# Two states per GpSimd product, channel-major tiles from the convolution, dt products in two row groups, and the skip term in two halves

## What is computed

```python
xz = x @ w_in.T
xi, z = jnp.split(xz, 2, axis=-1)                 # 256 channels each
xc = silu(depthwise_conv3x3(xi) + conv_b)
# four directions: by rows, by columns, and both of them backwards
x_dbl = jnp.einsum('bkdl,kcd->bkcl', xs, x_proj_w)        # 8 + 16 + 16 rows
dts, Bs, Cs = jnp.split(x_dbl, [8, 24], axis=2)
dts = jnp.einsum('bkrl,kdr->bkdl', dts, dt_w)
delta = softplus(dts + dt_b)
# along the 65536 tokens of a direction, for each of 16 states n:
h = exp(delta * A[n]) * h + delta * x * B[n]
y = sum_n(h * C[n]) + Ds * x
# the four y are added in the order of the picture, normed, gated by silu(z)
out = x + (layernorm(y) * silu(z)) @ w_out.T
```

## Time and profile before

| | |
|---|---|
| median of 3 runs | 27252.67 us (27248.71 to 27273.89) |
| profiled execution, span | 27255.4 us |
| VectorE (DVE) busy | 25541.9 us, 94% |
| TensorE (PE) busy | 24154.8 us, 89% |
| ScalarE (ACT) busy | 23950.4 us, 88% |
| GpSimd (POOL) busy | 22732.5 us, 83% |

### The profile page before, as it was taken

How to read it: one execution, slowest core, us unless ns; L and a number is a source line. 1 busy time by engine, 2 the same in 40 slices (tenths; PEclk the granted TensorE clock), 3 DMA queues, 4 the chain that set the end, 5 groups by cost and what they waited for, 6 DMA issues and landing times. The chain is left out here.

```text
span 27255.4 us, 517756 instructions
## 1 busy us (share of the span) xinstructions
PE 24154.8 (89%) x189836; PEld 20228.8 (74%) x189836; DVE 25541.9 (94%) x25237; ACT 23950.4 (88%) x47871; POOL 22732.5 (83%) x17291
## 2 busy tenths in 40 slices
PE   3998789999999989999999888888888888888889
PEld 1776457777777777777777777777777777777777
DVE  7999999999999999999999999999999999999996
ACT  2777459999999999999999999999999999999996
POOL 0000029999999999999999999999999999999996
PEclk7999899999999999999999999999999999999999
DMA  4112333333333344444444434344444444444435
GB/s 162 51 52 75 94 102 134 134 133 135 133 134 132 134 143 148 144 147 144 147 145 146 141 140 142 141 141 142 142 141 140 145 148 144 148 146 145 148 136 199
DMA packets 1529381, 3677.49 MB, mean 135 GB/s; under 512 B 105908, under 2 KB 1156952, under 8 KB 1247192
## 3 DMA queue, kind: packets, MB, share of 16 engines
q1 hardware_dynamic: 1526872, 3644.42, 38.3%
HBM read 3055.75 MB, written 588.25 MB: 134 GB/s over the span
## 5 line engine op out<-in xcount | busy, mean ns | idle before, releaser
L1198 POOL TENSOR_TENSOR s_prod<-s_h,s_cb 128x1024 f32<-128x1024 f32 x8192 | 19555.5, 2387 | 537.3 <-DVE s_h L1166 384.6
L1166 DVE TENSOR_TENSOR_SCAN s_h<-s_da,s_h,s_db 128x512 f32<-128x512 f32 x16256 | 19365.7, 1259 | 534.5 <-PE s_db L1070 497.4
L1127 ACT ACTIVATE s_da<-s_delta,a_neg 128x512 f32<-128x512 f32 x16384 | 10856.6, 712 | 1100.6 <-DVE s_h L1166 1100.4
L1116 ACT ACTIVATE s_dxb<-s_dx,s_btok 128x256 f32<-128x256 f32 x24576 | 10621.5, 498 | 53.1 <-PEq L57 53.1
L1067 PE MATMUL s_db<-eye,s_dxb 128*128 128x128 f32 x49152 | 8273.2, 277 | 2195.0 <-issue 1419.1
L1067 PEld LDWEIGHTS s_db<-eye,s_dxb 128*128 128x128 f32 x49152 | 5605.3, 142 | 4356.4 <-issue 3152.6
L1083 PE MATMUL s_py<-eye,s_prod 128*128 128x128 f32 x65536 | 8494.6, 273 | 10.2 <-POOL s_prod L1198 9.7
L1083 PEld LDWEIGHTS s_py<-eye,s_prod 128*128 128x128 f32 x65536 | 7432.8, 142 | 13.0 <-POOL s_prod L1198 13.0
L1070 PE MATMUL s_db<-s_bdiag,s_dx 128*128 128x128 f32 x32768 | 6338.9, 275 | 0.0
L1070 PEld LDWEIGHTS s_db<-s_bdiag,s_dx 128*128 128x128 f32 x32768 | 4951.9, 191 | 0.0
L1183 POOL TENSOR_SCALAR s_bdiag<-eye,s_btok 128x128 f32<-128x128 f32 x8192 | 3172.1, 387 | 226.9 <-POOLq L57 226.9
(11 more groups left out here) (132 smaller groups left out, 16852.9 us busy)
## 6 DMA issues: line engine op xcount, KB each, us to landing
s_cb<-c_rows SPq DMA_DIRECT2D x2048, 1024.0 KB, 4.7
s_xt<-xc_tok SPq DMA_DIRECT2D x1024, 256.0 KB, 5.3
y<-s_yt SPq DMA_DIRECT2D x1024, 256.0 KB
s_yb<-y SPq DMA_DIRECT2D x768, 256.0 KB, 4.5
xc_own<-s_xc SPq DMA_DIRECT2D x256, 512.0 KB, 3.4
s_xc<-xc_own SPq DMA_DIRECT2D x256, 512.0 KB, 5.6
xc_tok<-c_ot SPq DMA_DIRECT2D x32, 2048.0 KB, 8.5
o_y<-y SPq DMA_DIRECT2D x64, 1024.0 KB, 6.2
```

What stands on the lines that cost most here:

```text
L1116: last = e.activation(dxb[:, i % NDXB, j, :], dx[:, g % 2, j, :], ACT.Copy, scale=btok[:, g % 2, j, n:n + 1])
L1127: last = e.activation(da[:, i % NDA, half, :], delta[:, g % 2, half, :], ACT.Exp, scale=wts[k]["a_neg"][:, half, n:n + 1])
L1166: last = e.tensor_tensor_scan(h[:, n, half, flow], da[:, i % NDA, half, flow], db[:, i % NDB, half, flow], first, ALU.mult, ALU.add)
L1198: e.tensor_tensor(prod[:, i % NP_], h[:, n], cb[:, n, :].unsqueeze(1).to_broadcast([P, HALVES, T]), ALU.mult).then_inc(S["prod"], 1)
```

## The change

In `scans_phase`:

- GpSimd multiplies the two states of a pair (TOGETHER = 2) in one instruction of 2048 elements a partition; prod has three buffers of two states. Its scalings stay single and are issued up to two pairs ahead. A product waits for both scans. LAG goes from 2 to 4, so totals and y come two steps later; AHEAD stays 2.
- Only direction 1 (`turned_in`) transposes its tiles and stores them. Direction 0 reads channel-major tiles from xc_own[0], as the backward directions do.
- The projection has 73 output rows: the 9 rows of dt once more from row 64 on. Both halves of dt are formed in stage 6, the first from rows 0 to 8, the second from rows 64 to 72 of low and of dt_w, each into its own bank.
- The skip term's two halves of the channels are divided: half 0 in direction 2, half 1 in direction 3.
- Stage 11 waits for the token-major tile itself, since stage 0 is no longer there to do it.

In `conv_phase`, SP stores eight finished rows of xc to xc_own[0] in two DMAs (one a half) ahead of the store of xc_tok, and ScalarE waits for these stores before it writes the ring again.

```diff
+DT_AGAIN = ROWS_LOW
+ROWS_ALL = DT_AGAIN + DT_RANK + 1
...
+        def kept_again(e, r):
+
+            if r >= RING:
+                e.wait_ge(S[f"own{r // 8 % 2}"], HALVES * DMA * (r // RING))
...
+                        finished(e, r)
+                        tiles = slice((r - 7) * SIDE // BANK, (r + 1) * SIDE // BANK)
+                        for half in range(HALVES):
+                            e.dma_start(xc_own[0, tiles, :, half, :].rearrange("t p f -> p t f"),
+                                        xc[:, half, here:here + 8, :].rearrange("p (t r) w -> p t (r w)", r=BANK // SIDE)
+                                        ).then_inc(S[f"own{r // 8 % 2}"], DMA)
...
+                        kept_again(e, PAIR * q)
...
+                            kept_again(e, STRIP * c)
...
-    NDA, NDXB, NDB, NP_ = 3, 3, 2, 3
-    AHEAD, LAG = 2, 2
+    NDA, NDXB, NDB = 3, 3, 2
+    TOGETHER, GROUPS_KEPT = 2, 3
+    AHEAD, LAG = 2, 4
     SUBS_ACT = 3
     STEPS = TILES * D_STATE
-    SKIP = 2
+    SKIP = {2: 0, 3: 1}
     backwards = lambda k: k >= 2
     by_column = lambda k: k % 2 == 1
+    turned_in = lambda k: k == 1
...
-        prod = m.sb("s_prod", [P, NP_, HALVES, T])
+        prod = m.sb("s_prod", [P, GROUPS_KEPT, TOGETHER, HALVES, T])
...
-                    last = e.matmul(pr[0:ROWS_LOW, 0, :], w["proj"][:, half, :], xc[:, s, half, :],
+                    last = e.matmul(pr[0:ROWS_ALL, 0, :], w["proj"][:, half, :], xc[:, s, half, :],
...
-                e.matmul(pr[:, 0, :], w["dt_w"][:, 0:P], low[0:DT_RANK + 1, :], start=True, stop=True).then_inc(S["dts"], 1)
             elif stage == 6:
                 e.wait_ge(S["btok"], n)
-                e.matmul(pr[:, 1, :], w["dt_w"][:, P:2 * P], low[0:DT_RANK + 1, :], start=True, stop=True).then_inc(S["dts"], 1)
+                for half, at in enumerate((0, DT_AGAIN)):
+                    rows = slice(at, at + DT_RANK + 1)
+                    e.matmul(pr[:, half, :], w["dt_w"][rows, half * P:(half + 1) * P], low[rows, :],
+                             start=True, stop=True).then_inc(S["dts"], 1)
...
                 e.wait_ge(S["delta"], n)
+                e.wait_ge(S[f"load{s}"], LINES * DMA * ((n + 1) // 2))
...
+                e.dma_start(xc[:, 0], own(0, 0)).then_inc(S["xld0"], DMA)
                 load(e, 0, 0)
-                e.wait_ge(S["xc"], 1)
-                e.dma_start(own(0, 0), xc[:, 0]).then_inc(S["xst0"], DMA)
...
-                if not backwards(place(g)[0]):
+                if turned_in(place(g)[0]):
                     return 0
-                return (g + 1) // 2 if backwards(k) else 1
+                return 1 if turned_in(k) else (g + 1) // 2
+
+            def turns(g):
+
+                return g if turned_in(k) else 1
...
-                e.wait_ge(S["prod"], i + 1)
+                e.wait_ge(S["prod"], i // TOGETHER + 1)
...
-                        if k == SKIP and t >= 2:
+                        if k in SKIP and t >= 2:
                             e.wait_ge(S["skipped"], t - 1)
-                        if not backwards(k):
+                        if turned_in(k):
...
-                                last = e.matmul(out, prod[:, i % NP_, half, j * P:(j + 1) * P], const["eye"][:, :], start=first,
+                                last = e.matmul(out, prod[:, i // TOGETHER % GROUPS_KEPT, i % TOGETHER, half, j * P:(j + 1) * P], const["eye"][:, :], start=first,
...
-                        if n == 0 and k == SKIP:
+                        if n == 0 and k in SKIP:
+                            half = SKIP[k]
                             for j in range(SUBS):
-                                for half in range(HALVES):
-                                    out = py[:, j // 2, (j % 2) * D_INNER + half * P:(j % 2) * D_INNER + (half + 1) * P]
-                                    last = e.matmul(out, xc[:, g % 2, half, j * P:(j + 1) * P], wts[k]["d_diag"][:, half, :],
-                                                    start=False, stop=False, skip_group_check=True)
+                                out = py[:, j // 2, (j % 2) * D_INNER + half * P:(j % 2) * D_INNER + (half + 1) * P]
+                                last = e.matmul(out, xc[:, g % 2, half, j * P:(j + 1) * P], wts[k]["d_diag"][:, half, :],
+                                                start=False, stop=False, skip_group_check=True)
...
-                    for i in range(AHEAD):
-                        scale(i)
-                    for i in range(STEPS):
-                        g, n = divmod(i, D_STATE)
-                        if i + AHEAD < STEPS:
-                            scale(i + AHEAD)
+                    def product(p):
+                        g, n = divmod(TOGETHER * p, D_STATE)
+                        states = slice(n, n + TOGETHER)
                         if n % GROUP == 0:
                             c_loaded(e, g, n // GROUP)
-                        e.wait_ge(S["h"], i + 1)
-                        if i >= NP_:
-                            e.wait_ge(S["summed"], i - NP_ + 1)
-                        e.tensor_tensor(prod[:, i % NP_], h[:, n], cb[:, n, :].unsqueeze(1).to_broadcast([P, HALVES, T]),
+                        e.wait_ge(S["h"], TOGETHER * (p + 1))
+                        if p >= GROUPS_KEPT:
+                            e.wait_ge(S["summed"], TOGETHER * (p - GROUPS_KEPT + 1))
+                        e.tensor_tensor(prod[:, p % GROUPS_KEPT], h[:, states],
+                                        cb[:, states, :].unsqueeze(2).to_broadcast([P, TOGETHER, HALVES, T]),
                                         ALU.mult).then_inc(S["prod"], 1)
+
+                    for i in range(2 * TOGETHER):
+                        scale(i)
+                    for p in range(STEPS // TOGETHER):
+                        for i in range(TOGETHER * (p + 2), TOGETHER * (p + 3)):
+                            if i < STEPS:
+                                scale(i)
+                        product(p)
...
+        proj[k, :, B_ROW:ROWS_LOW] = xp[k, DT_RANK:].T
+        for at in (0, DT_AGAIN):
+            proj[k, :, at:at + DT_RANK] = xp[k, :DT_RANK].T
+            dt_w[k, at:at + DT_RANK] = w["L1_conv_dt_w"][k].T
+            dt_w[k, at + DT_RANK] = w["L1_conv_dt_b"][k]
```

More of the change, by code:

```diff
@@ L652, in _ @@
                     e.wait_ge(S[f"store{s}"], DMA * (ROWS // 8 // 2))
+                    e.wait_ge(S[f"own{s}"], HALVES * DMA * (ROWS // 8 // 2))
             @block.tensor
@@ L783, in scans_phase @@
         xc = m.sb("s_xc", [P, 2, HALVES, T])
-        low = m.sb("s_low", [ROWS_LOW, T])
+        low = m.sb("s_low", [ROWS_ALL, T])
         btok = m.sb("s_btok", [P, 2, SUBS, D_STATE])
@@ L841, in load_c, with prepare_pe @@
             e.dma_start(cb[:, q * GROUP:(q + 1) * GROUP, :], rows).then_inc(S[f"cl{q}"], DMA)
-        def prepare_pe(e, w, kept, g, n, stage, alone):
+        def prepare_pe(e, w, kept, turns, g, n, stage):
             s = g % 2
             if stage == 0 and not kept:
-                e.wait_ge(S[f"load{s}"], LINES * DMA * (1 if alone else (n + 1) // 2))
+                e.wait_ge(S[f"load{s}"], LINES * DMA * ((n + 1) // 2))
                 if n > 1:
@@ L869, in prepare_pe @@
                 for j in range(SUBS):
-                    last = e.transpose(pr[:, 1, j * ROWS_LOW:(j + 1) * ROWS_LOW], low[:, j * P:(j + 1) * P],
+                    last = e.transpose(pr[:, 1, j * ROWS_LOW:(j + 1) * ROWS_LOW], low[0:ROWS_LOW, j * P:(j + 1) * P],
                                        const["eye"][0:ROWS_LOW, 0:ROWS_LOW])
                 last.then_inc(S["turnb"], 1)
-                e.matmul(pr[:, 0, :], w["dt_w"][:, 0:P], low[0:DT_RANK + 1, :], start=True, stop=True).then_inc(S["dts"], 1)
             elif stage == 6:
                 e.wait_ge(S["btok"], n)
-                e.matmul(pr[:, 1, :], w["dt_w"][:, P:2 * P], low[0:DT_RANK + 1, :], start=True, stop=True).then_inc(S["dts"], 1)
+                for half, at in enumerate((0, DT_AGAIN)):
+                    rows = slice(at, at + DT_RANK + 1)
+                    e.matmul(pr[:, half, :], w["dt_w"][rows, half * P:(half + 1) * P], low[rows, :],
+                             start=True, stop=True).then_inc(S["dts"], 1)
             elif stage == 10:
@@ L883, in prepare_pe, with leave_turned @@
                 last.then_inc(S["turnd"], 1)
-        def leave_turned(e, copy, g, n):
-            e.wait_ge(S["turned"], n)
-            if n >= 3:
-                e.wait_ge(S[f"xst{g % 2}"], DMA * ((n - 1) // 2))
+        def leave_turned(e, copy, g, turns):
+            e.wait_ge(S["turned"], turns)
+            if turns >= 3:
+                e.wait_ge(S[f"xst{g % 2}"], DMA * ((turns - 1) // 2))
             copy(xc[:, g % 2], pr[:, :, :]).then_inc(S["xc"], 1)
@@ L909, in prepare_act, with prepare_dve @@
                 e.activation(e1(s), e1(s), ACT.Ln, bias=1.0).then_inc(S["log"], 1)
-        def prepare_dve(e, w, kept, g, n, stage):
+        def prepare_dve(e, w, kept, turns, g, n, stage):
```

(17 more changed lines are left out.)

23 lines of the change are left out of this document (11 added, 12 removed).

## The result

| | before | after |
|---|---|---|
| median of the runs | 27253.24 us (27248.71 to 27273.89) | 26460.42 us (26457.83 to 26464.39) |
| ratio of the two | | 0.9709, interval 0.9695 to 0.9722 |
| profiled execution, span | 27255.4 us | 26462.6 us |
| one tile, mean of 127, directions 0, 1, 2, 3 | 43.80, 43.79, 45.15, 43.67 us | 42.45, 42.59, 42.45, 42.45 us |

The change gains 793 us, 2.9%.

A forecast was written before the change was run, and what follows sets the result against it. GpSimd was taken to bound the scans, with VectorE near its limit. 27255.4 - 547 (tiles) + 12 (direction ends) + 5 (stores) - 3 (first tile) = 26722, forecast 26720 us, range 26400 to 26960.

The forecast's parts named there:

- GpSimd's loop of 0.6: Kernel before, once a tile: GpSimd waits 0.60 us through product of state 15, scaling, TensorE, total(15), y, scan, product.
- the chain: TensorE's turn, total, projection, turn, total between scan 17's end and y: 6.29 us, against 4.79 for VectorE's scans 18 and 19.
- Rival C: GpSimd's two-state product costs more per element through its operand's extra dimension; at 10% more, 28620 us; chance 0.07.
- GpSimd's floor: Scans: GpSimd's least time a tile, eight pairs of 5.24 us, 41.9 us instead of 43.0.
- Rival B: GpSimd stays the meter: a pair costs twice the single, tile 43.4 us, time 26900 us; chance 0.13.
- The wait ahead of y: VectorE idles about 1.5 us ahead of y in every tile (0.6 in direction 1), released by TensorE's totals.
- Rival A: No y wait forms; VectorE's own work is the tile, 41.5 and 42.5 us, time 26060; 0.15 with times up to the forecast.
- The waits at states 6 and 8: VectorE's idle of 0.21 and 0.35 us behind states 5 and 7 goes, as TensorE catches up during y's wait.
- in either case nothing is charged: TensorE's dt pair, 1.05 us side by side or 2.0 one behind the other, costs 0; up to 0.95 a tile without cover.
- The skip term: TensorE, halved over directions 2 and 3, now behind y's wait: direction 2's 1.22 us idle goes, direction 3 gains no wait.
- The convolution: New stores charged +5 us for the last only; the scans' first tile, without transposes and line 890's copy, -3 us.
- Rival D: The convolution's new stores (67 MB) are not hidden: up to +226 us, 26950 us; chance 0.05.

The follow-up runs named there:

- the kernel with the later preparation: Changed kernel with preparation stages 2 to 11, projection included, issued two steps later on TensorE, ScalarE and VectorE: 26155.65 us, ratio 0.9595.
- the two-singles kernel: Changed kernel with each pair's product as two one-state instructions, keeping its GpSimd order (two scalings ahead, then both products): 26666.10 us, ratio 0.9784.
- the doubled projection: Changed kernel with TensorE forming the next tile's projection twice in the scan loops: 27332.66 us, ratio 1.0025.
- the fastest kernel: Changed kernel with preparation stages 2 to 11 issued two steps later, so the projection no longer stands between scan 17 and y: 26155.65 us.
- the pairs alone: Kernel before with only two-state products, three buffers of pairs, LAG 4 and the new GpSimd order, without the other three parts: 26753.41 us, ratio 0.9813.

## Why the prediction was right, and where it was off

*GpSimd's pair.* Estimated 4600 ns and 5.24 a pair, measured 4563 and 5.21; the price per element from three sizes held at a fourth. The 4497 ns of the Trainium skill (GPSIMD Engine Reference, section 3) is 1.5% under this kernel's 4563. But the cheaper product carries only 206 of the 793 us. The prediction had GpSimd's loop of 0.6 give way to the chain and did not ask what the order of the scalings does; with the old order LAG 4 is slower than before. Rival C, an operand that costs more, is out: the longest product took 4617.

*GpSimd's floor.* 41.9 predicted, 41.7 measured. It is not reached in after; the kernel with the later preparation reaches it. Rival B is out for after, and the two-singles kernel is what it looks like when true. There too VectorE waits ahead of y for totals (1.8), so the sign that I had given for B, a wait for line 1183, would not have told it.

*The wait ahead of y.* 1.5 and 0.6 predicted, 1.35 and 0.36 measured, and its cause is shown by the doubled projection. Part of the closeness is luck: I had set 4.79 for scans 18 and 19 here and 4.70 in the tile sum; with 4.70, which is measured, it would have been 1.59, too long by about as much as the chain below. Rival A (no wait forms) is out for the same reason; with the projection moved away the time comes within 100 us of A's 26060.

*The tile was mis-sized:* 43.0 and 43.15 predicted, 42.45 and 42.59 measured. The savings a tile are 1.35, 1.20, 2.70 and 1.22, together 6.47 and not 4.31; times 127 that is 822 and not 547 us, 275 more, which covers the whole difference of 260. It has two terms. The first is the chain, 6.29 from the end of scan 17 to y: measured 0.15 + 5.86 + 0.04 = 6.04. Here "73 instead of 64 output rows, 0 to 0.26, I take 0" had the wrong sign. The bound reached only upwards, and the rows show the wider projection to be cheaper by 0.28 a tile. The second is VectorE's stretch from y to the end of the next scan 17: 36.7 predicted, 36.44 measured. I had returned only two overlaps of 0.09. In the earlier trace rows 12 scans take 14.38, in the fastest kernel 14.15: a fifth of a microsecond of waiting lay inside a group of scans whose line shows no idle time. The 0.15 by which direction 1 was to be later holds, 42.59 against 42.45. So the time came out between the forecast and rival A, where I had put 0.15; A's mechanism has no part in it, and a range drawn only as wide as the forecast's own terms would have missed.

*The waits at states 6 and 8* went as predicted, and the two dt records stand side by side. But "in either case nothing is charged" was wrong. One behind the other they cost 0.36 a tile. I had weighed 4.7 us of TensorE's work against 4.8 of scans, a margin of 0.1 in a sum of four rounded estimates. Only because the pair did run side by side did this not touch the forecast.

*The skip term.* No wait in direction 2 or 3, as predicted, but halving it was not needed. Of that direction's 2.7 us a tile (45.15 to 42.45), half comes with the pairs and the later totals alone (43.77), which take the skip term out of the projection's step; the rest comes once the dt product has left step 4 and the projection is wider, and the run with the skip term whole has the time of after.

*The convolution* was predicted at +5 and -3. From its first transpose on TensorE (2780.3 before, 2796.0 after) to the first scan (3950.7, 3964.8) it takes 1170.4 us before and 1168.8 after: -1.6 against +2 in sum. The stores are hidden: in the stretch that answers to the earlier trace rows the DMA share rises from 0.32 to 0.47 and VectorE stays at 193.6 of 200 us. Rival D is out.

```profile
3400.00:3600.00 200.00, 173.97 (x593) 95.67 (x594) 193.59 (x159) 94.99 (x149) 1.55 (x1) 0.95 0.47 152
```

*The ends of directions.* 3 us each predicted. From the last y of one direction to the first of the next it is 9469.8 - 9408.7 = 61.1 us, where it was 57.0, so 4.1. It stands at the start and not at the end, since the first y comes two states later: 4.1 in directions 0 and 1, 3.1 and 4.3 in 2 and 3, 15.5 in all against 12, and behind the last y of all nothing is added.

*Not foreseen:* the start. VectorE's first work comes 9.3 us later than before (25.73 against 16.41), and 6.4 us more are lost by the start of the convolution. The first is in SP's queue. Before, after, and the kernel with a projection of 64 rows (start, us of issuing, work, count):

```profile
9.54 1.43 SPq L1467 DMA_DIRECT2D w_dt_w<-in_dt_w  x4
```

```profile
9.07 6.39 SPq L1496 DMA_DIRECT2D w_dt_w<-in_dt_w  x4
15.50 4.51 SPq L1496 DMA_DIRECT2D w_A_logs<-in_A_logs  x4
```

```profile
9.54 2.39 SPq L1496 DMA_DIRECT2D w_dt_w<-in_dt_w  x4
```

Loads of dt_w with 9 partitions were issued in 1.43 us for four; with 73 they take 6.39 and hold up the next ones; with 64 they take 2.39, and VectorE starts at 17.46. It is the number 73 and not the size: 64 partitions are only an eighth less. The Trainium skill (DMA: Bandwidth & Descriptors, section "Why a DMA increments its semaphore by 16 and not by 1") says that a copy runs on the largest number of DMA engines, up to 16, that divides the count of its slowest dimension on both sides, here the partitions: one for 73, 16 for 64. The traces agree: from 10 to 15 us, while these loads run, the share of the 16 DMA engines is 0.08 in after and 0.36 with 64. Padding to a multiple of 16 would give back some 8 us, an estimate from VectorE's start at 25.73 and 17.46. Most of the 6.4 us need not be the change's: the pairs alone, whose code is that of before up to the scans and whose VectorE starts as early (16.38), also comes to the convolution 5.0 us later than before (2785.3).

Sum by these steps: 26722, less 275 for the tiles, plus 15.7 for the start, less 3.6 for the convolution, plus 3.5 for the ends, is 26463, against a span of 26462.6.

## What to carry to other kernels

Before an engine is made faster, work out the chain that will end last in its place, in the order in which the engines issue: here it gave the wait to 0.15 us (0.24 in direction 1), and it also named the next step, to move what stands in that chain (the projection) two steps away, worth another 305 us. Where an engine works off its instructions in the order of its program, look at how far ahead the small one stands that others wait for: the same instructions of GpSimd in two orders were 911 us apart. And try the change without its main idea: single products in the new order had 587 of the 793 us. A cover with a margin of 0.1 us in 4.8 is no cover, and an unknown cost should be bounded below zero as well.

## What the runs showed of the hardware that was not expected

A projection of 64 output rows among operations of 128 is dearer on TensorE than one of 73: from the total ahead of it to the next turn 0.97 + 1.86 before against 0.87 + 1.72 after, and 0.28 us a tile in the pair of runs that differ only in this width and what hangs on it (the copy to low, the loads of weights). TensorE's weight loads show where. Before, in direction 3 (64 rows), then after (73 rows):

```profile
24003.74 0.14 PEld L864 LDWEIGHTS s_pr<-s_xc,w_proj 128*64 128x64 f32 x1 [0.29 <-issue]
24004.69 0.31 PEld L1067 LDWEIGHTS s_db<-eye,s_dxb 128*128 128x128 f32 x3 [0.81 <-issue]
```

```profile
24042.17 0.14 PEld L882 LDWEIGHTS s_pr<-s_xc,w_proj 128*73 128x73 f32 x1 [0.28 <-issue]
24042.60 0.14 PEld L1090 LDWEIGHTS s_db<-eye,s_dxb 128*128 128x128 f32 x1 [0.28 <-issue]
```

Behind 73 columns the next transpose's weights are loaded 0.43 us ahead of its product (24042.60, 24043.03), while the last product of the projection still runs. Behind 64 columns that load starts with its own product (24004.69 both). Why the load is not drawn ahead there, no run here shows.

With a load's partitions the number matters more than the size: at 1 KB a partition, four loads of 73 partitions took 6.39 us to issue, four of 64 took 2.39 and four of 9 took 1.43.

The dt products of both halves (four records of 9 rows), from partitions 0 and 64, take 1.13 us side by side and 1.98 one behind the other; one half alone took 1.12, so the second is almost free.
